# Attention and quantised projection on one core: the max pass leads the exponentials by ten units instead of six, and the query/key projection takes another slot

## The chip, the core and the metric

The kernel runs on one core of one Trainium2 chip. The metric is the time of one execution on the device in microseconds (us), as the median of several runs. The core's engines are TensorE (PE, with its weight loads PEld), VectorE (DVE), ScalarE (ACT), GpSimd (POOL) and SyncE (SP), whose queue here issues every DMA.

## The reference

For each of 16 sequences of 256 tokens with 128 features (float32):

```python
qkv = x @ attn_w.T + attn_b                      # 16 heads of 8, split into q, k, v
scores = einsum("bhki,bhqi->bhkq", k, q) / sqrt(8)
probs = softmax(where(key <= query, scores, -10000), axis=keys)
x = layernorm(x + combine(probs, v) @ out_w.T + out_b)
q_lhs, q_rhs = int8 roundings of x and rhs by absmax / 127
x = layernorm(x + (q_lhs @ q_rhs) * lhs_scale * rhs_scale)
```

## The kernel before

A **batch** b is one sequence. The scores of a batch are made twice on TensorE, in twelve **units** u = 0 to 11 of two or four head pairs and one block of 64 keys each. The **max pass** (`scores_for_max`, bf16, written as M here) puts a unit into one of two PSUM banks `max_bank`; VectorE reduces it (`maxima`, L608), and after the twelfth unit it joins the partial maxima (`join_maxima`, L616). TensorE transposes them (`turn_maxima`, L833), VectorE makes the negated shift of each query from them in three steps (`make_shift`, L632, L638, L641), and SP copies the shift into four extra rows of `q_move` (`load_shift`, L310). The **exp pass** (`scores_for_exp`, written as E) multiplies again with these rows in, into one of three banks `exp_bank`; ScalarE takes the exponential (L453), and TensorE multiplies with the values (`pv`, L819, eight groups 0 to 7).

Queries and keys are split into three bf16 parts so that the score products are accurate. TensorE projects (`project_qk`, L846, into `bank_b`), ScalarE copies the result out twice for each of q and k (`qk_from_psum`, L469: `qk_parts` and `qk_f`, w = 0 and 1), GpSimd subtracts the first part (`split(b, False)`, L393, gives `qk_rest`), VectorE rounds the second part and copies the first one again (`second_part`, L622 and L623), and GpSimd subtracts once more (`split(b, True)`, L397). SP writes the parts to an image in DRAM in two halves (`write_image`, L287) and reads it back in the order that the score products want (`read_image`, L300 and L301). The semaphore `qk_split` counts four steps of a batch.

Behind the attention come `pv_from_psum` (L487), `turn_pv` (L882, into `bank_b`), `normalise` (L651, L655), `turn_heads` (L894), `heads_from_psum` (L494), `project_out` (L902), the first norm, the rounding (`round_z`, L510), `turn_zq` (L915), `zq_from_psum` (L518), `feed_forward` (L923), `scale_ffn` (L703), and the second norm.

The order on each engine is written out by hand. All five engines run the same loop over **phases** b. In phase b, slot u, TensorE issues the max unit `max_unit(b, u)` and the exp unit u of batch b, and behind them what the slot lists; the other engines list their work by the same slots. Each engine takes its own list strictly in order, so an instruction that waits holds back all that stands behind it. With a lead of six, phase b holds units 6 to 11 of the max pass of batch b + 1 in slots 0 to 5 and units 0 to 5 of batch b + 2 in slots 6 to 11. Before the first exp pass come phases -3 to -1 with set-up, ten warm-up matmuls and one more behind each max unit (L941).

Of the kernel before, what the change touches and what calls it, by code (L numbers as in the profile page):

```python
# [46 lines left out]
PARTS = 3  # L47
# [22 lines left out]
HALF = NU // 2  # L70
# [11 lines left out]
def phases(phase, before={}):  # L82

    for b in range(-3, NBATCH + 3):
        if b in before:
            before[b]()
        phase(b)


def max_unit(b, u):  # L90

    return (b + 1, u + HALF) if u < HALF else (b + 2, u - HALF)


def build_program(nc, x, xt, wqkv_t, bqkv, wo_t, bo, rhs_t, out):
    ctx = ExitStack()
    with ctx:
# [30 lines left out]
        ones_b = sb("ones_b", [2, TOK], BF16)  # L128
# [6 lines left out]
        qk_parts = sb("qk_parts", [128, len(PART_SLOTS), TOK], BF16)  # L135

        part = [qk_parts[:, 2 - n:6 + n:3 + 2 * n, :] for n in range(PARTS)]
        first_again = qk_parts[:, 3:5, :]
# [109 lines left out]
        POOL_FIRST = 8 + 2 + (QK_RING - 1) + (QK_RING - 2)  # L248
        POOL_SETUP = POOL_FIRST + 3 * RING
# [5 lines left out]
        def _(sp):  # L255
# [22 lines left out]
            def write_image(b, half):  # L278
# [6 lines left out]
                for w in range(2):  # L285
                    at = RUNS[w][half]
                    sp.dma_start(image[w][b % QK_RING][:, 3 * half:3 * half + 3, :],  # L287
                                 qk_parts[:, at:at + 3, :]).then_inc(image_written[b % QK_RING], 16)
# [62 lines left out]
        def _(pool):  # L351
# [21 lines left out]
            for i in range(1, QK_RING):  # L373
                step(pool.memset(q_move[i][:, :, :].bitcast(F32), 0.0))
            for i in range(2, QK_RING):
                step(pool.memset(k_stat[i][:, :, :, :].bitcast(F32), 0.0))
            assert done[0] == POOL_FIRST, done[0]

# [8 lines left out]
            def split(b, last):  # L387

                if not real(b) or b == 0:
                    return  # L390
                if not last:
                    wait(pool, qk_out, b)
                    pool.tensor_tensor(qk_rest[:, :, :], qk_f[:, :, :], part[0],  # L393
                                       ALU.subtract).then_inc(qk_split[1], 1)
                else:
                    wait(pool, qk_split, b, 3)
                    pool.tensor_tensor(part[2], qk_rest[:, :, :], part[1],  # L397
# [47 lines left out]
        def _(act):  # L445
# [10 lines left out]
            def qk_from_psum(b, w):  # L456
# [8 lines left out]
                for dst in (part[0][:, w, :], qk_f[:, w, :]):  # L465
# [68 lines left out]
            def v_columns_stand():  # L534
# [475 lines left out]
```

## Time and profile before

| what | value |
|---|---|
| median of 3 runs | 300.79 us (300.47 to 301.21) |
| the profiled execution, own time | 302.37 us |
| its span in the trace | 300.7 us |
| granted TensorE clock, mean over the span | 0.962 |
| busy: PE, DVE, ACT, POOL | 248.0, 198.7, 188.5, 112.1 us |

The span is what the trace covers; the execution's own time has 1.67 us more around it. A busy share is an average over a fill, a steady part and a drain. The exp pass of batch 0 starts 40.37 us into the span, that of batch 15 at 266.54 us.

### The profile page before, as it was taken

What the parts mean: (1) busy time and instruction counts of PE and PEld (TensorE: products, weight loads), DVE (VectorE), ACT (ScalarE), POOL (GpSimd) and SP (SyncE); (2) the same over time, 40 slices, a digit from 0 to 9 for tenths busy, and PEclk for the clock granted to TensorE, in tenths of its full rate; (3) what the DMA queues carried; (4) which work ended last, traced back from release to release, by engine and by line L of the source; (5) the groups of instructions that cost most, each with busy time, mean ns of one, the idle gap of its engine ahead of it and who ended that gap; (6) DMA issues with size and microseconds to landing.
All of it is one profiled execution on the core that took longest, in us unless ns stands there. A gap on an engine that the chain in (4) does not pass through costs nothing.

```text
span 300.7 us, 8257 instructions
## 1 busy us (share of the span) xinstructions
PE 248.0 (82%) x3073; PEld 170.2 (57%) x3073; DVE 198.7 (66%) x561; ACT 188.5 (63%) x434; POOL 112.1 (37%) x218
## 2 busy tenths in 40 slices
PE   2389588898989898999899999999998999989410
PEld 1236365666666566666566666666666667655300
DVE  7827558394959685867676767768595978733421
ACT  4023046657677685858594958676777767787441
POOL 7931103123243342525243444443434342433342
PEclk9999899999999999999999999999999999999655
DMA  2356583736373538163815664374636361010000
GB/s 88 109 109 181 118 193 111 142 108 143 109 142 124 143 102 168 65 142 87 197 45 159 109 182 84 127 144 141 125 126 123 127 127 39 2 37 20 19 17 19
DMA packets 51000, 32.72 MB, mean 109 GB/s; under 512 B 7312, under 2 KB 50960, under 8 KB 50960
## 3 DMA queue, kind: packets, MB, share of 16 engines
q1 hardware_dynamic: 50960, 32.19, 43.8%
q8 instruction: 24, 0.39, 0.6%
q14 instruction: 16, 0.13, 0.2%
HBM read 17.17 MB, written 14.68 MB: 106 GB/s over the span
## 4 chain that ended last, share of the span: by engine, by line
PE 26%; SPq 15%; ACT 14%; DMA 14%; DVE 13%; issue 13%; POOL 4%; ACTq 0%; DVEq 0%; POOLq 0%
DMA q_move<-shift 9%; SPq L287 8%; PE exp_bank L776 5%; PE bank_b L846 5%; PE pv_bank L819 4%; ACT probs L453 4%; DVE part_max L608 4%; ACT qk_f L469 3%; PE max_bank L776 3%; PE bank_b L882 3%; ACT heads_t L487 2%; SPq L310 2%; DVE key_max L616 2%; ACT qk_parts L469 2%; DMA k_stat<-imagek 2%
## 5 line engine op out<-in xcount | busy, mean ns | idle before, releaser
L608 DVE TRANSPOSE_TENSOR_REDUCE part_max<-max_bank 128x16 f32<-128x512 f32 (+1 forms) x192 | 119.3, 625 | 69.9 <-PE max_bank L779 65.6
L453 ACT ACTIVATE probs<-exp_bank 128x512 f32<-128x512 f32 (+1 forms) x192 | 102.5, 535 | 74.5 <-PE exp_bank L779 73.1
L776 PE MATMUL exp_bank<-q_move,k_stat 128*128 128x128 bf16 (+3 forms) x512 | 67.5, 234 | 9.1 <-DMA q_move<-shift 9.1
L776 PE MATMUL max_bank<-q_move,k_stat 124*128 124x128 bf16 (+3 forms) x512 | 71.1, 241 | 4.1 <-DMA k_stat<-imagek 3.6
L819 PE MATMUL pv_bank<-probs,v_stat 128*32 128x256 f32 (+3 forms) x1024 | 61.1, 311 | 0.0
L776 PEld LDWEIGHTS max_bank<-q_move,k_stat 124*128 124x128 bf16 x512 | 40.0, 118 | 32.3 <-issue 11.5
L776 PEld LDWEIGHTS exp_bank<-q_move,k_stat 128*128 128x128 bf16 x512 | 41.5, 114 | 15.3 <-DMA q_move<-shift 11.0
L779 PE MATMUL max_bank<-causal,identb 128*128 128x128 bf16 (+1 forms) x192 | 46.3, 241 | 0.0
L779 PE MATMUL exp_bank<-causal,identb 128*128 128x128 bf16 (+1 forms) x192 | 45.5, 237 | 0.0
L393 POOL TENSOR_TENSOR qk_rest<-qk_f,qk_parts 128x512 f32<-128x512 f32 x15 | 17.4, 1159 | 45.2 <-ACT qk_f L469 45.2
L469 ACT ACTIVATE qk_parts<-bank_b,bias 128x256 bf16<-128x256 f32 x32 | 21.3, 665 | 20.6 <-DMA imagek<-qk_parts 16.9
L397 POOL TENSOR_TENSOR qk_parts<-qk_rest,qk_parts 128x512 bf16<-128x512 f32 x15 | 17.4, 1160 | 37.5 <-DVE qk_parts L623 37.5
L819 PEld LDWEIGHTS pv_bank<-probs,v_stat 128*32 128x32 f32 x1024 | 20.2, 108 | 17.3 <-issue 8.8
L415 POOL TENSOR_SCALAR rstd<-moments 128x2 f32<-128x2 f32 x32 | 6.2, 193 | 56.0 <-DVE moments L677 47.6
L428 POOL TENSOR_TENSOR r<-ffn,z 128x256 f32<-128x256 f32 x16 | 11.7, 728 | 36.5 <-DVE ffn L703 36.5
L846 PE MATMUL bank_b<-xt_in,wqkv 128*128 128x256 f32 x64 | 19.3, 428 | 6.0 <-DMA wqkv<-wqkv_dram 3.7
L417 POOL TENSOR_TENSOR rstd<-rstd,minus_half 128x2 f32<-128x2 f32 x32 | 22.6, 705 | 2.7
L469 ACT ACTIVATE qk_f<-bank_b,bias 128x256 f32<-128x256 f32 x32 | 19.9, 623 | 0.0
L527 ACT ACTIVATE o<-r,rstd 128x128 f32<-128x128 f32 x32 | 13.9, 485 | 8.6 <-POOL rstd L421 8.6
L779 PEld LDWEIGHTS max_bank<-causal,identb 128*128 128x128 bf16 x192 | 19.0, 99 | 0.1
L779 PEld LDWEIGHTS exp_bank<-causal,identb 128*128 128x128 bf16 x192 | 18.8, 98 | 0.0
L882 PE MATMUL bank_b<-ident,heads_t 128*128 128x128 f32 x64 | 10.4, 285 | 10.2 <-ACT heads_t L487 10.2
(84 smaller groups left out, 313.4 us busy)
## 6 DMA issues: line engine op xcount, KB each, us to landing
imageq<-qk_parts SPq DMA_DIRECT2D x32, 192.0 KB, 2.1
imagek<-qk_parts SPq DMA_DIRECT2D x32, 192.0 KB, 2.1
q_move<-imageq SPq DMA_DIRECT2D x32, 192.0 KB, 3.7
k_stat<-imagek SPq DMA_DIRECT2D x32, 192.0 KB, 4.2
xt_in<-xt_dram SPq DMA_DIRECT2D x16, 128.0 KB, 4.5
x_in<-x_dram SPq DMA_DIRECT2D x16, 128.0 KB, 4.2
out_dram<-o SPq DMA_DIRECT2D x16, 128.0 KB, 2.0
q_move<-shift SPq DMA_DIRECT2D x32, 8.0 KB
```

What stands on the lines that cost most here:

```text
L287: sp.dma_start(image[w][b % QK_RING][:, 3 * half:3 * half + 3, :], qk_parts[:, at:at + 3, :]).then_inc(image_written[b % QK_RING], 16)
L393: pool.tensor_tensor(qk_rest[:, :, :], qk_f[:, :, :], part[0], ALU.subtract).then_inc(qk_split[1], 1)
L397: pool.tensor_tensor(part[2], qk_rest[:, :, :], part[1], ALU.subtract).then_inc(qk_split[1], 1)
L417: pool.tensor_tensor(t[:, 0, :], t[:, 0, :], minus_half[:, :], ALU.pow).then_inc(made[1], 1)
L453: act.activation(probs[u][:, 0:cols], exp_bank[u % EXP_BANKS][:, 0:cols], ACT.Exp, scale=SCALE).then_inc(exp_done[1], 1)
L469: act.activation(dst, src, ACT.Identity, bias=bias[:, w:w + 1]).then_inc(qk_out[1], 1)
L608: dve.tensor_reduce(o32, max_bank[u % MAX_BANKS][:, 0:n * (TOK - key)].rearrange("k (c q) -> k c q", q=32), op=ALU.max, axis=AX.X, apply_t ...
L776: pe.matmul(tiles[:, j, :], keys, q_move[b % QK_RING][0:rows, p0 + j, key:TOK], start=(j == 0), stop=False, skip_group_check=True)
L779: return pe.matmul(tiles[:, :, 0:KB], identb[:, :], causal[:, :].unsqueeze(1).to_broadcast([128, n, KB]), start=False, stop=True, skip_gro ...
L819: last = pe.matmul(pv_bank[col:col + 32, g, key:TOK], v_stat[b % RING][:, key // KB, p0 + j, :], tiles_of(probs[u], u)[:, j, :], start=(n ...
L846: last = pe.matmul(bank_b[:, w * TOK:(w + 1) * TOK], wqkv[:, w, :], xt_in[b % XT_RING][:, :], start=(w == 0), stop=True, skip_group_check= ...
L882: last = pe.transpose(bank_b[:, c:c + 128], heads_t[:, g, t * 128:(t + 1) * 128], ident[:, :])
```

## The change

The maximum pass leads by ten units: phase b holds units 10 and 11 of batch b + 1 in slots 0 and 1 and units 0 to 9 of batch b + 2 behind them. `turn_maxima` moves from slot 7 to 2, `make_shift` to slots 3 and 4. `project_qk` moves from slot 0 (for batch b + 3) to slot 9 (for b + 4), its copies on ScalarE to slots 10 and 11, `second_part` on VectorE from slot 6 to slot 0 of the next phase. `qk_parts` exists twice. The second copy of the first part (L623) moves from VectorE to GpSimd, and `second_part` waits for it (`qk_split` 2 of 4). SP's list is re-ordered. The rows of ones in `k_stat` come by one DMA for each of the four buffers, from a tile that GpSimd prepares, instead of four each. Other slots move as shown. The cut diff:

```diff
-HALF = NU // 2
+LEAD = 10
...
-    for b in range(-3, NBATCH + 3):
+    for b in range(-4, NBATCH + 3):
...
-    return (b + 1, u + HALF) if u < HALF else (b + 2, u - HALF)
+    ahead, unit = divmod(u + LEAD, NU)
+    return b + 1 + ahead, unit
...
-        ones_b = sb("ones_b", [2, TOK], BF16)
+        shift_on = sb("shift_on", [128, 2, TOK], BF16)
...
-        qk_parts = sb("qk_parts", [128, len(PART_SLOTS), TOK], BF16)
-
-        part = [qk_parts[:, 2 - n:6 + n:3 + 2 * n, :] for n in range(PARTS)]
-        first_again = qk_parts[:, 3:5, :]
+        qk_parts = [sb(f"qk_parts{i}", [128, len(PART_SLOTS), TOK], BF16) for i in range(2)]
+
+        part = [[qk_parts[i][:, 2 - n:6 + n:3 + 2 * n, :] for n in range(PARTS)] for i in range(2)]
+        first_again = [qk_parts[i][:, 3:5, :] for i in range(2)]
...
-        POOL_FIRST = 8 + 2 + (QK_RING - 1) + (QK_RING - 2)
-        POOL_SETUP = POOL_FIRST + 3 * RING
+        POOL_FIRST = 14
+        POOL_ROWS = POOL_FIRST + 2 * (QK_RING - 2)
+        POOL_SETUP = POOL_ROWS + 3 * RING
...
+            def set_shift_rows(slots):
+
+                for i in slots:
+                    sp.dma_start(k_stat[i][SHIFT_ROW:DEPTH, :, :, :],
+                                 shift_on[SHIFT_ROW:DEPTH, :, :].unsqueeze(1).to_broadcast([4, PAIRS, 2, TOK])).then_inc(ones_loaded, 16)
+
             def rows_stand():
 
-                sp.wait_ge(rows_set, 3)
-                load_ones((0, 1))
-                sp.wait_ge(pool_setup, 1)
+                sp.wait_ge(rows_set, 2)
+                sp.wait_ge(pool_setup, POOL_FIRST)
+                set_shift_rows((0, 1))
 
             def last_rows_stand():
-                sp.wait_ge(pool_setup, POOL_FIRST)
-                load_ones(range(2, QK_RING))
-
-            def load_ones(slots):
-
-                for i in slots:
-                    for s in range(2):
-                        for row in (SHIFT_ROW + s, SHIFT_ROW + 2 + s):
-                            sp.dma_start(k_stat[i][row:row + 1, :, s, :],
-                                         ones_b[0:1, :].unsqueeze(1).to_broadcast([1, PAIRS, TOK])).then_inc(ones_loaded, 16)
+                sp.wait_ge(pool_setup, POOL_ROWS)
+                set_shift_rows(range(2, QK_RING))
 
             def phase(b):
-                load_xt(b + 4)
                 load_x(b)
                 write_image(b + 3, 0)
-                store(b - 3)
                 write_image(b + 3, 1)
                 load_shift(b + 1)
+                load_xt(b + 5)
                 read_image(b + 3)
-
-            phases(phase, {-3: rows_stand, -2: last_rows_stand})
+                store(b - 3)
+
+            phases(phase, {-3: rows_stand, -1: last_rows_stand})
...
+            step(pool.memset(shift_on[:, :, :], 0.0))
+            for row in (SHIFT_ROW, SHIFT_ROW + 2):
+                step(pool.affine_select(out=shift_on[:, :, :], in_=shift_on[:, :, :], compare_op=ALU.not_equal, fill=1.0,
+                                        base=-row, pattern=[[-1, 2], [0, TOK]], channel_multiplier=1))
+            step(pool.memset(q_move[1][:, :, :].bitcast(F32), 0.0))
             assert done[0] == POOL_FIRST, done[0]
+
+            def last_rows():
+                for i in range(2, QK_RING):
+                    step(pool.memset(q_move[i][:, :, :].bitcast(F32), 0.0))
+                    step(pool.memset(k_stat[i][:, :, :, :].bitcast(F32), 0.0))
+                assert done[0] == POOL_ROWS, done[0]
...
+                first, second, third = part[b % 2]
                 if not last:
                     wait(pool, qk_out, b)
-                    pool.tensor_tensor(qk_rest[:, :, :], qk_f[:, :, :], part[0],
+                    wait(pool, qk_split, b - 1)
+                    pool.tensor_tensor(qk_rest[:, :, :], qk_f[:, :, :], first,
                                        ALU.subtract).then_inc(qk_split[1], 1)
+                    pool.tensor_copy(first_again[b % 2], first).then_inc(qk_split[1], 1)
...
+                norm_factors(b - 2, 0, y_made, rstd_made)
+                split(b + 3, True)
                 add_residual(b - 3)
-                split(b + 3, False)
+                add_bias(b - 1)
                 norm_factors(b - 3, 1, r_stats, rstd2_made)
-                split(b + 3, True)
-                add_bias(b - 1)
-                norm_factors(b - 1, 0, y_made, rstd_made)
-
-            phases(phase, {-2: rest_of_setup, 1: sum_stands})
+                split(b + 4, False)
+
+            phases(phase, {-3: last_rows, -1: rest_of_setup, 1: sum_stands})
...
-                    wait(act, qk_split, b - 1)
-                    wait_ring(act, image_written, b - 1, 4, 4)
+                    wait(act, qk_split, b - 1, 1)
+                    wait_ring(act, image_written, b - 2, 4, 4)
...
+                if b == 0:
+                    act.wait_ge(pool_setup, POOL_SETUP)
...
-                    if u == 1:
-                        qk_from_psum(b + 3, 0)
+                    if u == 0:
+                        zq_from_psum(b - 3)
                     if u == 2:
-                        qk_from_psum(b + 3, 1)
+                        norm1(b - 2)
                     if u == 3:
                         pv_from_psum(b - 1)
                     if u == 4:
-                        norm1(b - 2)
-                    if u == 5:
                         v_from_psum(b + 1)
-                    if u == 6:
-                        norm2(b - 3)
                     if u == 7:
+                        round_z(b - 2)
+                    if u == 8:
                         heads_from_psum(b - 1)
                     if u == 9:
-                        round_z(b - 2)
+                        norm2(b - 3)
+                    if u == 10:
+                        qk_from_psum(b + 4, 0)
                     if u == 11:
-                        zq_from_psum(b - 2)
-
-            phases(phase, {-1: v_columns_stand})
+                        qk_from_psum(b + 4, 1)
+
+            phases(phase)
...
-                    wait(dve, qk_split, b, 1)
-                    dve.tensor_copy(part[1], qk_rest[:, :, :]).then_inc(qk_split[1], 1)
-                    dve.tensor_copy(first_again, part[0]).then_inc(qk_split[1], 1)
-
+                    wait(dve, qk_split, b, 2)
+                    dve.tensor_copy(part[b % 2][1], qk_rest[:, :, :]).then_inc(qk_split[1], 1)
...
-                    if u == HALF:
+                    maxima(*max_unit(b, u))
+                    if u == 0:
+                        first_sum(b - 2, 2)
+                        if b > -3:
+                            second_part(b + 3)
+                    if u == 1:
                         join_maxima(b + 1)
-                    maxima(*max_unit(b, u))
-                    if u == 0 and b == -2:
-                        second_part(b + 3)
-                    if u == 1:
+                    if u == 2:
                         scale_ffn(b - 3)
                     if u == 3:
+                        make_shift(b + 1, 0)
+                        make_shift(b + 1, 1)
+                    if u == 4:
+                        make_shift(b + 1, 2)
+                        scales(b - 2, 0)
+                    if u == 5:
                         second_stats(b - 3, 0)
-                    if u == 4:
+                        scales(b - 2, 1)
+                    if u == 6:
+                        normalise(b - 1, 0)
                         second_stats(b - 3, 1)
-                    if u == 5:
-                        normalise(b - 1, 0)
-                        scales(b - 2, 0)
+                        scales(b - 2, 2)
                         normalise(b - 1, 1)
-                    if u == 6:
-                        scales(b - 2, 1)
-                        if b >= -1:
-                            second_part(b + 3)
-                    if u == 7:
-                        make_shift(b + 1, 0)
-                        scales(b - 2, 2)
-                        make_shift(b + 1, 1)
-                    if u == 8:
-                        make_shift(b + 1, 2)
-                    if u == 9:
+                    if u == 10:
                         first_sum(b - 1, 0)
-                    if u == 10:
+                    if u == 11:
                         first_sum(b - 1, 1)
-                    if u == 11:
-                        first_sum(b - 1, 2)
...
-                if real(b - 2):
-                    wait(pe, normed, b - 2)
-                else:
+                if real(b + 2):
                     wait(pe, qk_out, b + 2)
+                else:
+                    wait(pe, normed, b - 3)
...
+                if real(b - 5):
+                    wait(pe, normed, b - 5)
+                elif real(b - 3):
...
-                if real(b + 4):
-                    wait(pe, qk_out, b + 4)
-                elif real(b + 1):
-                    wait(pe, shift_made, b + 1)
+                if real(b + 2):
+                    wait(pe, shift_made, b + 2)
...
-                    if b == -2 and u == HALF:
-                        setup()
-                        warm_up(WARM)
                     scores_for_max(*max_unit(b, u))
                     scores_for_exp(b, u)
-                    if b == -1 or (b == -2 and u >= HALF):
+                    if b == -1 or (b == -2 and u >= NU - LEAD):
                         warm_up(1)
                     if u == 0:
                         pv(b - 1, 5)
-                        feed_forward(b - 3)
-                        project_qk(b + 3)
                     if u == 1:
                         pv(b - 1, 6)
+                        feed_forward(b - 3)
                     if u == 2:
+                        turn_maxima(b + 1)
                         pv(b - 1, 7)
                     if u == 3:
                         project_v(b + 1)
-                    if u == 4:
+                    if u == 5:
                         turn_pv(b - 1)
-                    if u == 5:
                         pv(b, 0)
                     if u == 6:
                         pv(b, 1)
+                    if u == 7:
                         turn_heads(b - 1)
-                    if u == 7:
-                        turn_maxima(b + 1)
                         pv(b, 2)
-                    if u == 8:
+                    if u == 9:
                         project_out(b - 1)
-                    if u == 9:
+                        project_qk(b + 4)
                         pv(b, 3)
                     if u == 10:
                         pv(b, 4)
                     if u == 11:
                         turn_zq(b - 2)
 
+            def setup_and_warm_up():
+                setup()
+                warm_up(WARM)
+
             pe.wait_ge(w_in, 16)
-            phases(phase)
+            phases(phase, {-2: setup_and_warm_up})
```

## Rows read from the trace of the kernel before

**Rows 1.** The page, first part: busy us (share) xinstructions of each engine.
```profile
PE 248.0 (82%) x3073; PEld 170.2 (57%) x3073; DVE 198.7 (66%) x561; ACT 188.5 (63%) x434; POOL 112.1 (37%) x218
```
**Rows 2.** Waits, 100 to 235 us: who <- for whom: us, times, longest.
```profile
PE bank_b L882 <- ACT heads_t L487: 6.5, 9, 0.7
PE exp_bank L776 <- DMA q_move<-shift: 5.4, 8, 1.0
```
**Rows 3.** Timeline of PE: start us, us; first exp units of batches 1, 12, 13, 14.
```profile
52.71 0.41 PE L776 MATMUL exp_bank<-q_move,k_stat 128*128 128x256 bf16 x2 [0.87 <-DMA q_move<-shift]
...
225.51 0.41 PE L776 MATMUL exp_bank<-q_move,k_stat 128*128 128x256 bf16 x2 [0.56 <-DMA q_move<-shift]
...
241.36 0.41 PE L776 MATMUL exp_bank<-q_move,k_stat 128*128 128x256 bf16 x2 [0.69 <-DMA q_move<-shift]
...
254.51 0.38 PE L776 MATMUL exp_bank<-q_move,k_stat 128*128 128x256 bf16 x2
```
**Rows 4.** The chain of waits, 144 to 179 us: start us, us, what.
```profile
147.84 0.92 PE bank_b L846 x4
```
**Rows 5.** Timeline of PE: from `turn_zq` to group 7 of `pv`.
```profile
254.01 0.38 PE L915 MATMUL bank_a<-ident,zq 128*128 128x128 f32 x2
...
257.03 0.32 PE L819 MATMUL pv_bank<-probs,v_stat 128*32 128x64 f32 x8
```
**Rows 6.** Timeline: exp of a last unit; copies of keys; GpSimd's first subtraction.
```profile
60.20 0.64 PE L819 MATMUL pv_bank<-probs,v_stat 128*32 128x256 f32 x8
...
60.37 0.38 ACT L453 ACTIVATE probs<-exp_bank 128x256 f32<-128x256 f32 x1 [0.80 <-PE exp_bank L779]
60.65 0.77 ACT L480 ACTIVATE v_stat<-bank_a 64x256 f32<-64x256 f32 x2
...
150.99 0.86 ACT L469 ACTIVATE qk_parts<-bank_b,bias 128x256 bf16<-128x256 f32 x1
...
151.55 0.77 ACT L469 ACTIVATE qk_f<-bank_b,bias 128x256 f32<-128x256 f32 x1
...
152.40 1.16 POOL L393 TENSOR_TENSOR qk_rest<-qk_f,qk_parts 128x512 f32<-128x512 f32 x1 [1.31 <-ACT qk_f L469]
```
**Rows 7.** Timeline of DVE, 154 to 158 us.
```profile
154.12 0.45 DVE L608 TRANSPOSE_TENSOR_REDUCE part_max<-max_bank 128x8 f32<-128x256 f32 x1 [1.11 <-PE max_bank L779]
...
155.01 0.41 DVE L655 TENSOR_TENSOR heads<-bank_b,rden 128x256 f32<-128x256 f32 x1
...
155.34 0.60 DVE L616 TENSOR_REDUCE key_max<-part_max 128x64 f32<-128x256 f32 x1
...
156.72 0.41 DVE L622 CAST qk_parts<-qk_rest 128x512 bf16<-128x512 f32 x1
...
157.05 0.29 DVE L623 COPY qk_parts<-qk_parts 128x512 bf16<-128x512 bf16 x1
```
**Rows 8.** Timeline of POOL: two operations with one input.
```profile
3.13 0.29 POOL L367 TENSOR_SCALAR_AFFINE_SELECT ident<-ident 128x128 f32<-128x128 f32 x1 [0.23 <-POOL minus_half L365]
...
153.64 0.19 POOL L415 TENSOR_SCALAR rstd<-moments 128x2 f32<-128x2 f32 x1
```
**Rows 9.** Timeline: the copy of the heads; one max unit to `turn_heads`.
```profile
157.54 0.38 ACT L494 ACTIVATE heads_d<-bank_a 128x256 f32<-128x256 f32 x1
...
247.63 0.41 PE L776 MATMUL max_bank<-q_move,k_stat 124*128 124x256 bf16 x2
...
248.76 0.44 PE L894 MATMUL bank_a<-ident,heads 128*128 128x128 f32 x2
```
**Rows 10.** Timeline of the fill: warm-up matmuls around TensorE's longest wait; GpSimd's filling of `v_stat`.
```profile
11.45 2.99 POOL L381 MEMSET v_stat<- 128x1024 f32 x3
...
29.83 0.38 PE L941 MATMUL exp_bank<-warm 128*128 128x512 bf16 x1
33.78 0.41 PE L776 MATMUL max_bank<-q_move,k_stat 124*128 124x256 bf16 x2 [3.58 <-DMA k_stat<-imagek]
...
35.47 0.63 PE L941 MATMUL exp_bank<-warm 128*128 128x512 bf16 x1
```

More of the change, by code:

```diff
@@ L287, in write_image @@
                     sp.dma_start(image[w][b % QK_RING][:, 3 * half:3 * half + 3, :],
-                                 qk_parts[:, at:at + 3, :]).then_inc(image_written[b % QK_RING], 16)
+                                 qk_parts[b % 2][:, at:at + 3, :]).then_inc(image_written[b % QK_RING], 16)
             def read_image(b):
@@ L372, in _ @@
                                         base=0, pattern=[[-1, KB]], channel_multiplier=1))
[L373 to L376, printed above, removed]
-            assert done[0] == POOL_FIRST, done[0]
+            step(pool.memset(shift_on[:, :, :], 0.0))
[3 more added lines that the diff above has]
+            step(pool.memset(q_move[1][:, :, :].bitcast(F32), 0.0))
+            assert done[0] == POOL_FIRST, done[0]
+            def last_rows():
[3 more added lines that the diff above has]
+                assert done[0] == POOL_ROWS, done[0]
             def rest_of_setup():
@@ L390, in split @@
                     return
+                first, second, third = part[b % 2]
                 if not last:
                     wait(pool, qk_out, b)
-                    pool.tensor_tensor(qk_rest[:, :, :], qk_f[:, :, :], part[0],
+                    wait(pool, qk_split, b - 1)
+                    pool.tensor_tensor(qk_rest[:, :, :], qk_f[:, :, :], first,
                                        ALU.subtract).then_inc(qk_split[1], 1)
+                    pool.tensor_copy(first_again[b % 2], first).then_inc(qk_split[1], 1)
                 else:
                     wait(pool, qk_split, b, 3)
-                    pool.tensor_tensor(part[2], qk_rest[:, :, :], part[1],
+                    pool.tensor_tensor(third, qk_rest[:, :, :], second,
                                        ALU.subtract).then_inc(qk_split[1], 1)
@@ L461, in qk_from_psum @@
                     wait(act, qk_proj, b)
-                    wait(act, qk_split, b - 1)
-                    wait_ring(act, image_written, b - 1, 4, 4)
+                    wait(act, qk_split, b - 1, 1)
+                    wait_ring(act, image_written, b - 2, 4, 4)
                 src = bank_b[:, w * TOK:(w + 1) * TOK]
-                for dst in (part[0][:, w, :], qk_f[:, w, :]):
+                for dst in (part[b % 2][0][:, w, :], qk_f[:, w, :]):
                     if w == 1:
@@ L532, in _ @@
             act.wait_ge(bias_in, 16)
-            def v_columns_stand():
-                act.wait_ge(pool_setup, POOL_SETUP)
             def phase(b):
@@ L568, in _ @@
             dve.memset(warm[:, :].bitcast(F32), 0.0).then_inc(warm_zeroed, 1)
-            dve.memset(ones_b[:, :], 1.0).then_inc(rows_set, 1)
             for i in range(2):
@@ L572, in _ @@
             dve.memset(part_max[:, :, :], MASKED).then_inc(rows_set, 1)
-            dve.wait_ge(rows_set, 4)
+            dve.wait_ge(rows_set, 3)
             def rhs_scales():
@@ L745, in phase @@
-                    if u == 8:
-                        make_shift(b + 1, 2)
-                    if u == 9:
+                    if u == 10:
                         first_sum(b - 1, 0)
-                    if u == 10:
+                    if u == 11:
                         first_sum(b - 1, 1)
-                    if u == 11:
-                        first_sum(b - 1, 2)
-            first = 0
             rhs_scales()
-            wait(dve, qk_out, first)
-            dve.tensor_tensor(qk_rest[:, :, :], qk_f[:, :, :], part[0],
+            wait(dve, qk_out, 0)
@@ L759, in _ @@
+            dve.tensor_tensor(qk_rest[:, :, :], qk_f[:, :, :], part[0][0],
                               ALU.subtract).then_inc(qk_split[1], 1)
-            second_part(first)
-            wait(dve, qk_split, first, 3)
-            dve.tensor_tensor(part[2], qk_rest[:, :, :], part[1],
+            dve.tensor_copy(first_again[0], part[0][0]).then_inc(qk_split[1], 1)
+            second_part(0)
+            wait(dve, qk_split, 0, 3)
+            dve.tensor_tensor(part[0][2], qk_rest[:, :, :], part[0][1],
@@ L798, in scores_for_exp @@
                     if b == 0:
-                        pe.wait_ge(ones_loaded, 16 * 4 * QK_RING)
+                        pe.wait_ge(ones_loaded, 16 * QK_RING)
                     pe.wait_ge(shift_loaded, 32 * (b + 1))
@@ L827, in turn_maxima @@
                 wait(pe, max_joined, b)
-                if real(b - 2):
-                    wait(pe, normed, b - 2)
+                if real(b + 2):
+                    wait(pe, qk_out, b + 2)
                 else:
-                    wait(pe, qk_out, b + 2)
+                    wait(pe, normed, b - 3)
                 for s in range(2):
@@ L840, in project_qk @@
                 wait_ring(pe, xt_loaded, b, 1)
-                if real(b - 3):
+                if real(b - 5):
+                    wait(pe, normed, b - 5)
+                elif real(b - 3):
                     wait(pe, shift_made, b - 3)
```

## The prediction

> **What bounds the kernel now.** I read the page first: TensorE is the busiest engine with 82% of the span, VectorE has 66% [rows 1]. A share over fill and drain says little, so I took the waits of the steady part next. TensorE has two kinds of wait there: for the shift rows that SP copies, just ahead of each exp pass (5.4 us in 8 times), and for ScalarE's copy ahead of `turn_pv` (6.5 us in 9 times) [rows 2]. Then I measured a phase by the start of its first exp unit: phase 12 takes 225.51 to 241.36 = 15.85 us; phases 1 to 11 take (225.51 - 52.71) / 11 = 15.71 each; phase 13, the first with nothing to project for queries and keys, takes 254.51 - 241.36 = 13.15 [rows 3]. In phase 13 TensorE hardly waits. The projection costs TensorE 0.92 [rows 4]. So TensorE's own work is 13.15 + 0.92 = 14.07 us a phase, and 1.6 us of each full phase are waits. That is what any re-ordering can win: some 12 x 1.6 = 20 us. The reader is to see that the kernel sits close to the bound of one engine whose list is taken in order: whatever it waits for is paid in full.
>
> **What the change takes away.** The maxima of batch b + 1 are joined in slot 1 of phase b, the shift is made by slot 4 and needed a phase later, so the wait for the shift rows goes. `turn_pv` waited because `qk_from_psum` stood in front of `pv_from_psum` on ScalarE (its wait on `qk_out`); these copies are now in slots 10 and 11, so that wait goes as well. If nothing took their place the phase would be 14.07.
>
> **What the change puts in their place.** Follow the parts of batch b + 3. ScalarE ends their copies in slot 11 of phase b - 1; GpSimd then subtracts and copies; VectorE's `second_part` stands in slot 0 of phase b, behind one max unit, and waits for both (`qk_split` 2). Queued behind it on VectorE are the reduction of max unit 11 and `join_maxima`, and TensorE's `turn_maxima` in slot 2 waits for the join. The chain, from the moment TensorE has issued exp unit 11:
> - ScalarE takes its exponential 0.17 later and is free for the next instruction after 0.28 (60.20, 60.37, 60.65); the first copy of the keys holds it 0.56 (150.99 to 151.55), the second lasts 0.77 [rows 6]: 1.78.
> - GpSimd starts 0.08 later and subtracts for 1.16 [rows 6]: 3.02.
> - GpSimd's copy of 512 bf16 elements is not in the trace. One-input operations take 0.19 for 2 elements and 0.29 for 128 [rows 8], 0.8 ns an element, so 0.60 for 512. Bounds: 0.29 (the one with a quarter of the elements) and 1.16 (the two-input one of the same size). I take 0.60, since it has one input: 3.62.
> - VectorE starts some 0.07 later, the cast holds it 0.33 (156.72 to 157.05), the reduction of unit 11 takes 0.45, the join 0.60 with 0.03 ahead of it [rows 7]: 5.10. TensorE starts 0.08 later: 5.18.
>
> In that time TensorE has `turn_zq`, three max and three exp units, two groups of `pv` and the feed-forward product: before, the same list takes 257.03 - 254.01 = 3.02 [rows 5]; with the somewhat larger max units that now fall there 3.1. So TensorE stands 5.18 - 3.1 = 2.1 us at `turn_maxima` in every phase from 0 to 12. A copy of 0.29 makes it 1.8, one of 1.16 makes it 2.6. The loop closes on itself: a later `turn_maxima` makes the next exp unit 11 later too, so nothing catches up.
>
> The GPSIMD Engine Reference of the Trainium skill, section on engine selection, says elementwise work belongs on VectorE and that GpSimd is slower, near line rate only with one input; that speaks against the moved copy. VectorE's copy takes 0.29 [rows 7], against my 0.60. By the same page's best case for a one-input loop, 512 elements in about 0.77 us, which no row here shows, the stall would be 2.2 to 2.3 and the whole 2 us more.
>
> **Smaller waits that come up.** `turn_heads` (slot 7) waits for VectorE's `heads`, made in slot 6. Before, from the start of the reduction to the end of `heads` it is 155.42 - 154.12 = 1.30 [rows 7], with one other operation between; after, the reduction is the 512-column one, 0.27 longer, and two small ones replace the other: 1.6, and with 0.31 ahead and 0.08 behind 2.0 us. TensorE covers it with an exp unit, a `pv` group, a smaller max unit and an exp unit: the first three take about 1.1 [rows 9], with the fourth 1.55. Stall 0.45. `project_out` (slot 9) waits for `heads_d`, which ScalarE now makes behind exponential 8 with nothing else on TensorE in slot 8: 0.3 + 0.38 for the exponential + 0.38 for the copy [rows 9] + 0.06 = 1.12 against 0.75 of TensorE's work: 0.4. `project_v` (slot 3) waits for `scale_ffn`, behind the delayed join: 0.1. Together 0.95 a phase, bounds 0 (all three covered) and 1.3.
>
> **Costed at nothing.** SP's new order: the image of a batch is written 3 to 6 us after the stall, read some 2 us later, and needed a phase later, about 6 us of cover; `store` at the end of the phase only holds back loads due later. The single DMAs for the ones, the tile behind them and the double `qk_parts` act in the fill. The four max units taken out of phases 14 and 15 give back 1.1 us.
>
> **Fill.** TensorE's wait of 3.58 for the second image [rows 10] shrinks, since the second batch's parts no longer wait for the first image. But `second_part` of batch 2 stands in front of max unit 11 of batch 0, so that TensorE waits from about 29.5 to 32.7; and GpSimd fills `v_stat` (2.99 [rows 10] and six small ones, 4.2) before the third part of batch 2, whose image lands only near 45.5. These times are estimates, the list of the fill gone through with the same durations. With the chain above once more in phase 0 the first exp unit of batch 1 moves from 52.71 to 56.3: +3.6, bounds 0 and +6.
>
> **The sum**, against the span of 300.7. A full phase: 14.07 + 2.1 + 0.95 = 17.1. Fill +3.6. Phases 1 to 11: 11 x 17.1 - 0.5 (no feed-forward in phase 1) = 187.6 against 172.8: +14.8. Phase 12: 17.1 - 0.92 = 16.2 against 15.85: +0.3. Phase 13: +0.9. Phases 14, 15 and the drain: -1.1. Together +18.5: span 319.2, its own time 1.67 more, 320.9. The profiled execution's 302.37 stands 1.6 over the median of the runs, 300.79, so the median becomes 319.3.
>
> **Rivals.**
> - *TensorE-bound, faster.* If the chain were hidden, the phase would be 14.07 + 0.95 = 15.0: fill +1.5, phases 1 to 11 -8, phase 12 -1.8, rest -0.2: 292; without the small waits 281. For it: both old waits do go. Against: the phase gets shorter only if the stall is under 15.71 - 15.0 = 0.7, the chain under 3.8 us; ScalarE's part, GpSimd's subtraction, the reduction and the join alone are 1.78 + 1.16 + 0.45 + 0.60 = 3.99, without the copy, the cast and every hand-over. Chance 0.10.
> - *Break-even.* The chain near 3.8 to 4.2 us, with some of the smaller waits gone: within 1 us of 300.8, or a few us over. 0.04 for the same.
> - *The clock falls.* A stall of about 1 us before each exp pass left the clock at 2.4 GHz; behind the wait of 3.58 a warm-up matmul takes 0.63 where it took 0.38 [rows 10], and it stays so for some 3 us, which costs about 1.6. My stalls of 2.1 lie between. If each did this: 12 x 1.6 = +19, 338. The skill's page TensorE: Matmul & The Clock Gate, section on oscillation, describes such a kernel that starts cold in each of its tiles; by it the time would be this 338 if the stall were long enough. 0.08.
> - *The small waits are covered*, the main stall stays: 319.3 - 12 = 307. This is the low side of the forecast.
>
> **Chances and range.** The stall at `turn_maxima`, clock kept: 0.78, from 304 (no small waits, a fill that loses nothing) to 329 (copy at 1.16, fill +6). The 0.10, 0.04 and 0.08 are the rest. Within 0.3% is what a measurement of this kernel can tell from no change. Slower 0.86, same 0.04, faster 0.10.
>
> **What the trace after would show.** Right: a wait of TensorE's `turn_maxima` for `join_maxima`, 2 us, once a phase; VectorE idle ahead of its cast for GpSimd's copy, 1.5 to 2 us; no wait for the shift rows; phases of 17.1. Wrong: phases near 14 to 15, with GpSimd's pair ending before VectorE gets to the cast; or matmuls at half speed behind each stall; or waits for the images.

## Result, and the profile after

The changed kernel takes 336.32 us (median of 4 runs, 335.71 to 337.17) against 300.89 for the kernel before on the same chip: ratio 1.118, 95% interval 1.115 to 1.121. The profiled execution spans 334.7 us. The forecast was slower, 319.3 us, in a range of 304 to 329: the direction and the place of the stall are right, the size is not.

The page of the changed kernel, first its busy shares and then the granted clock in 40 slices. Line numbers below are those of the changed kernel and of each experiment; they stand a few lines from those of before. TensorE's share falls from 82% [rows 1] to 79% though its busy time rises from 248.0 to 264.2 us on the same work. Some 10 us of that rise lie in the stretches at a lower clock, the sixes to eights in the clock's row: a phase with one keeps TensorE busy for 15.9 to 16.1 us, the others for 14.7.

```profile
PE 264.2 (79%) x3075; PEld 179.0 (53%) x3077; DVE 195.7 (58%) x545; ACT 189.3 (57%) x434; POOL 123.8 (37%) x236
...
PEclk9999769999998989997979999897979799999955
```

The waits of the changed kernel from 100 to 260 us (who <- for whom: us, times, longest). The two waits of [rows 2] are gone. In their place stands `turn_maxima` (L835) waiting for the join, and under it VectorE's cast (L630) waiting for GpSimd's copy.

```profile
DVE qk_parts L630 <- POOL qk_parts L404: 16.7, 8, 2.1
PE bank_b L835 <- DVE key_max L624: 14.0, 8, 1.8
PE bank_a L904 <- ACT heads_d L506: 3.7, 9, 0.4
PE bank_a L925 <- ACT zq_t L530: 1.7, 8, 0.2
PE bank_a L896 <- DVE heads L661: 1.4, 9, 0.2
PE bank_a L867 <- DVE ffn L709: 1.0, 5, 0.2
```

The timeline of the changed kernel from the end of exp unit 11 to `turn_maxima` (start us, us). The first row's start is the moment at which unit 11 has been issued; the rows behind it are the links of the predicted chain in order.

```profile
147.15 0.38 PE L917 MATMUL bank_a<-ident,zq 128*128 128x128 f32 x2
147.47 0.40 ACT L463 ACTIVATE probs<-exp_bank 128x256 f32<-128x256 f32 x1
147.73 0.86 ACT L479 ACTIVATE qk_parts<-bank_b,bias 128x256 bf16<-128x256 f32 x1
148.29 0.78 ACT L479 ACTIVATE qk_f<-bank_b,bias 128x256 f32<-128x256 f32 x1
149.15 1.16 POOL L402 TENSOR_TENSOR qk_rest<-qk_f,qk_parts 128x512 f32<-128x512 f32 x1 [6.62 <-ACT qk_f L479]
150.26 0.61 POOL L404 COPY qk_parts<-qk_parts 128x512 bf16<-128x512 bf16 x1
150.90 0.43 DVE L630 CAST qk_parts<-qk_rest 128x512 bf16<-128x512 f32 x1 [2.09 <-POOL qk_parts L404]
151.24 0.44 DVE L616 TRANSPOSE_TENSOR_REDUCE part_max<-max_bank 128x8 f32<-128x256 f32 x1
151.72 0.58 DVE L624 TENSOR_REDUCE key_max<-part_max 128x64 f32<-128x256 f32 x1
152.36 0.34 PE L835 MATMUL bank_b<-ident,key_max 128*64 128x64 f32 x4 [1.75 <-DVE key_max L624]
```

The chain is 152.36 - 147.15 = 5.21 us; 5.18 was worked out. GpSimd's copy is 0.61 against 0.60.

What was not in the sum comes right behind it. The windows of the changed kernel (stretch, busy us of each engine, PEclk, DMA share, GB/s), in the same phase:

```profile
147.10:152.30 5.20, 3.29 (x47) 2.18 (x43) 3.06 (x9) 3.65 (x9) 2.90 (x5) 1.00 0.10 31
152.30:154.50 2.20, 1.95 (x35) 1.49 (x36) 2.06 (x7) 1.72 (x4) 2.11 (x5) 0.94 0.45 164
154.50:157.90 3.40, 3.40 (x29) 2.60 (x28) 2.08 (x8) 1.76 (x5) 0.71 (x2) 0.54 0.38 125
157.90:165.00 7.10, 6.53 (x78) 4.48 (x78) 3.47 (x10) 3.68 (x9) 1.28 (x4) 1.00 0.74 148
```

For 3.4 us TensorE is at 1.2 GHz (PEclk 0.54, as the row's edges are a little off that stretch) and busy all the time. Two rows of its timeline show a pair of matmuls of one shape, ahead of the stall and in that stretch:

```profile
145.42 0.35 PE L778 MATMUL max_bank<-q_move,k_stat 124*128 124x192 bf16 x2
...
154.45 0.51 PE L778 MATMUL max_bank<-q_move,k_stat 124*128 124x192 bf16 x2
```

The stall is 1.75 us in each of phases 3 to 12. In phases 1 and 2 it is longer:

```profile
63.31 0.34 PE L835 MATMUL bank_b<-ident,key_max 128*64 128x64 f32 x4 [2.30 <-DVE key_max L624]
...
80.50 0.34 PE L835 MATMUL bank_b<-ident,key_max 128*64 128x64 f32 x4 [2.33 <-DVE key_max L624]
```

The exp pass, by the first exp unit of each batch: the start of batch 1 (us from the span's start), then lengths in us.

| | before | after | sum of the prediction |
|---|---|---|---|
| batch 1 | 52.71 | 58.51 | 56.3 |
| phases 1 to 11, each | 15.71 | 18.18 | 17.1 |
| phase 12 | 15.85 | 17.57 | 16.2 |
| phase 13 | 13.15 | 14.43 | 14.05 |
| batch 14 to the end | 46.2 | 44.2 | 45.1 |

The phases after are of two kinds: 17.1 to 17.5 us where the clock stays, 18.4 to 18.8 where one stretch of 3.4 us runs at 1.2 GHz. The second kind is 7 of phases 1 to 11 (3, 4, 6, 7, 9, 10 and 11); phase 12 has such a stretch too. Phases 1 and 2, with the longest stalls, have none.

### The profile page after: what moved, and what is told of

The parts are those of the page before. It is cut to its first block, busy times and chain, and to the rows that moved or that the text cites. A ratio compares the mean times of both kernels' runs of the same rounds, so it can differ in the third digit from the quotient of the medians.

```text
span 334.7 us, 8270 instructions
## 1 busy us (share of the span) xinstructions
PE 264.2 (79%) x3075; PEld 179.0 (53%) x3077; DVE 195.7 (58%) x545; ACT 189.3 (57%) x434; POOL 123.8 (37%) x236
## 3 DMA queue, kind: packets, MB, share of 16 engines
HBM read 17.17 MB, written 14.68 MB: 95 GB/s over the span
## 4 chain that ended last, share of the span: by engine, by line
PE 48%; DVE 14%; ACT 12%; issue 11%; POOL 10%; DMA 2%; SPq 1%; ACTq 0%; DVEq 0%; POOLq 0%
PE max_bank L778 9%; PE pv_bank L821 8%; PE exp_bank L778 6%; POOL qk_rest L402 4%; PE bank_b L850 4%; ACT qk_f L479 4%; PE bank_a L867 4%; PE bank_a L904 4%; ACT qk_parts L479 3%; DVE part_max L616 3%; PE bank_b L884 3%; PE exp_bank L781 3%; DVE key_max L624 2%; PE max_bank L781 2%; POOL qk_parts L404 2%
## 5 line engine op out<-in xcount | busy, mean ns | idle before, releaser
L616 DVE TRANSPOSE_TENSOR_REDUCE part_max<-max_bank 128x16 f32<-128x512 f32 (+1 forms) x192 | 117.3, 620 | 76.8 <-PE max_bank L781 74.3
L778 PE MATMUL max_bank<-q_move,k_stat 124*128 124x128 bf16 (+3 forms) x512 | 74.9, 250 | 4.1 <-DMA k_stat<-imagek 3.4
L778 PE MATMUL exp_bank<-q_move,k_stat 128*128 128x128 bf16 (+3 forms) x512 | 70.7, 244 | 0.0
L402 POOL TENSOR_TENSOR qk_rest<-qk_f,qk_parts 128x512 f32<-128x512 f32 x15 | 17.4, 1158 | 115.0 <-ACT qk_f L479 114.9
L778 PEld LDWEIGHTS max_bank<-q_move,k_stat 124*128 124x128 bf16 x512 | 38.3, 119 | 37.5 <-issue 15.5
L781 PE MATMUL max_bank<-causal,identb 128*128 128x128 bf16 (+1 forms) x192 | 48.1, 251 | 0.0
L781 PE MATMUL exp_bank<-causal,identb 128*128 128x128 bf16 (+1 forms) x192 | 47.4, 247 | 0.0
L778 PEld LDWEIGHTS exp_bank<-q_move,k_stat 128*128 128x128 bf16 x512 | 44.3, 118 | 4.7 <-issue 2.5
L425 POOL TENSOR_SCALAR rstd<-moments 128x2 f32<-128x2 f32 x32 | 8.7, 271 | 72.9 <-DVE moments L724 51.1
L630 DVE CAST qk_parts<-qk_rest 128x512 bf16<-128x512 f32 x16 | 9.1, 568 | 28.8 <-POOL qk_parts L404 28.8
L835 PE MATMUL bank_b<-ident,key_max 128*64 128x64 f32 x64 | 5.6, 257 | 25.0 <-DVE key_max L624 24.9
L513 ACT ACTIVATE z<-y,rstd 128x128 f32<-128x128 f32 x32 | 14.0, 487 | 19.4 <-POOL rstd L431 19.4
L407 POOL TENSOR_TENSOR qk_parts<-qk_rest,qk_parts 128x512 bf16<-128x512 f32 x15 | 17.4, 1160 | 3.6 <-DVE qk_parts L630 3.5
```

The source lines that it names most:

```text
L402: pool.tensor_tensor(qk_rest[:, :, :], qk_f[:, :, :], first, ALU.subtract).then_inc(qk_split[1], 1)
L407: pool.tensor_tensor(third, qk_rest[:, :, :], second, ALU.subtract).then_inc(qk_split[1], 1)
L513: act.activation(z[b % RING][:, t, :], y[:, t, :], ACT.Identity, bias=rstd[0][:, 1, t:t + 1], scale=rstd[0][:, 0, t:t + 1]).then_inc(z_mad ...
L616: dve.tensor_reduce(o32, max_bank[u % MAX_BANKS][:, 0:n * (TOK - key)].rearrange("k (c q) -> k c q", q=32), op=ALU.max, axis=AX.X, apply_t ...
L778: pe.matmul(tiles[:, j, :], keys, q_move[b % QK_RING][0:rows, p0 + j, key:TOK], start=(j == 0), stop=False, skip_group_check=True)
L781: return pe.matmul(tiles[:, :, 0:KB], identb[:, :], causal[:, :].unsqueeze(1).to_broadcast([128, n, KB]), start=False, stop=True, skip_gro ...
```

## Experiments

All are edits of the changed kernel that leave out none of its work. Each is timed beside the kernel before, which has 301.13 us beside the late `second_part`, the eight matmuls, the copy back and the small waits, and 301.03 beside the other four. "Undisturbed" is a phase without a stretch at 1.2 GHz.

**`second_part` two slots later** (`e1_second_late`).

```diff
 # VectorE
                     if u == 0:
                         first_sum(b - 2, 2)
-                        if b > -3:
+                        if b == -2:
                             second_part(b + 3)
...
                     if u == 2:
                         scale_ffn(b - 3)
+                        if b > -2:
+                            second_part(b + 3)
```

> The changed kernel with one edit: second_part moves from slot 0 to the end of slot 2 on VectorE (in the fill phase -2 it stays). Theory A (the stall of TensorE at turn_maxima, 1.8 us a phase, comes from second_part standing in front of the reduction of unit 11 and of the join; the clock falls only because of that stall): no wait of turn_maxima over 0.2 us, granted clock near 0.96, full phases of 15.0 to 15.2 us where the changed kernel has 17.4 to 18.8, time 290 to 298 us. Theory B (the ten-unit lead itself costs the time, through banks or shared engines): phases stay over 16.5 us and the time over 312 us.

311.5 us, ratio 1.034 (1.032 to 1.036). `turn_maxima` no longer waits at all, and from batch 1 to the drain no stretch is at 1.2 GHz; phases are 16.25 us. So both the stall and the clock hang on the place of this one call: 25 us of the 35 that the change costs. But 16.25 is 1.05 over theory A's 15.2, and the time misses its 298 by 13.5. The waits of this kernel, 100 to 240 us:

```profile
PE bank_b L886 <- ACT heads_t L499: 6.2, 8, 0.8
PE bank_a L906 <- ACT heads_d L506: 3.7, 9, 0.4
PE bank_a L927 <- ACT zq_t L530: 1.9, 9, 0.2
PE bank_a L898 <- DVE heads L661: 1.3, 8, 0.2
```

The wait for `heads_t` that the prediction struck off is back with 0.8 us a phase, once the larger stall no longer covers it.

**The stall filled with matmuls** (`e2_busy_stall`). Eight matmuls on a zero tile run while `turn_maxima` waits for the join, which comes no earlier.

```diff
 # turn_maxima(b)
+                if real(b + 2):
+                    wait(pe, qk_out, b + 2)
+                    for _ in range(8):
+                        pe.matmul(bank_b[:, :], warm[:, 0:128], warm[:, :], start=True, stop=True)
                 wait(pe, max_joined, b)
```

> The changed kernel with eight matmuls on a zero tile (some 1.7 us) in front of turn_maxima's wait for the join, into a bank that is free there; the stall itself stays. Theory A (behind the stall the granted clock falls to 1.2 GHz for 3.4 us in most phases, and that costs some 1.3 us each time): no stretch at half clock in the steady part, all full phases near 17.4 us, time 323 to 328 us, 8 to 13 us under the changed kernel, although work is added. Theory B (the slow matmuls are not due to the idle time): the stretches stay and the time is 336 us or more.

329.17 us, ratio 1.091 (1.087 to 1.095) against 1.118 for the changed kernel: 7 us less for 112 matmuls more; theory A's band of 323 to 328 is missed by one. From phase 3 on all full phases take 17.5 us. Timeline and windows of this kernel; the window's PEclk column is 1.00 in each phase:

```profile
149.71 1.89 PE L832 MATMUL bank_b<-warm 128*128 128x512 bf16 x8
151.64 0.34 PE L839 MATMUL bank_b<-ident,key_max 128*64 128x64 f32 x4
```
```profile
112.00:129.50 17.50, 16.44 (x201) 10.85 (x199) 11.14 (x35) 11.64 (x28) 7.00 (x13) 1.00 0.48 116
129.50:147.00 17.50, 16.45 (x202) 10.86 (x200) 11.14 (x34) 11.65 (x28) 7.00 (x13) 1.00 0.46 115
147.00:164.50 17.50, 16.44 (x201) 10.85 (x199) 11.13 (x34) 11.64 (x29) 7.01 (x13) 1.00 0.46 115
```

So the idle time in front of `turn_maxima` is what lowers the clock. The lower clock costs 200.0 - 191.9 = 8.1 us over phases 1 to 11 and 17.57 - 16.62 = 0.95 in phase 12.

**Four matmuls in its place** (`e7_half_busy`, the same edit with `range(4)`).

> As e2_busy_stall, with four zero matmuls instead of eight, so that about 0.9 us of idle time is left in front of turn_maxima's matmuls. Theory A (the clock falls for the length of the idle stretch, and one of about 1 us, as the kernel before had in each phase, is harmless): no half-clock stretch in the steady part, within 2 us of e2_busy_stall's 329 us. Theory B (any idle stretch there is enough now and then): some stretches stay, 331 to 336 us.

327.43 us, ratio 1.088 (1.086 to 1.090), phases of 17.49 us, no stretch at 1.2 GHz in the steady part: theory A. Of the 1.7 us under the kernel with eight, 1.6 are in the fill, where batch 1 starts at 58.37 and not at 60.01. TensorE's idle time ahead of `turn_maxima` is 7.1 us in 8 times, 0.9 each, and the clock stays up, as it did with the 0.7 to 1.0 of the kernel before [rows 2]. In phases 1 and 2 it is 1.44 and 1.47, and the clock stays up there too.

**The copy back on VectorE** (`e3_copy_back`).

```diff
 # GpSimd, split(b, False)
-                    pool.tensor_copy(first_again[b % 2], first).then_inc(qk_split[1], 1)
...
 # VectorE, second_part(b)
-                    wait(dve, qk_split, b, 2)
+                    wait(dve, qk_split, b, 1)
                     dve.tensor_copy(part[b % 2][1], qk_rest[:, :, :]).then_inc(qk_split[1], 1)
+                    dve.tensor_copy(first_again[b % 2], part[b % 2][0]).then_inc(qk_split[1], 1)
```

> The changed kernel with the second copy of the first part made on VectorE again, behind the cast, and second_part waiting only for GpSimd's subtraction. Theory A (everything in the chain counts in full): the chain is 0.61 us shorter on GpSimd and 0.25 longer on VectorE, so the stall goes from 1.8 to about 1.4 us and phases at full clock from 17.4 to 17.0; with half-clock stretches as frequent as in the changed kernel 331 us, with none 319 us. Theory B (the copy on GpSimd is the cause of the loss): the stall is under 0.5 us and the time under 310 us.

324.24 us, ratio 1.076 (1.072 to 1.081), between theory A's two ends. The stall is 1.40 us as expected, undisturbed phases are 17.13 for 17.0. In the profiled execution 3 of phases 1 to 12 have a stretch at 1.2 GHz, where it was 8: phases 1 and 2, whose stalls are longer, and of the ten with 1.40 us one, phase 12. The 0.35 us that the chain lost (0.6 less on GpSimd, the copy more on VectorE) come off the stall in full, and with the fewer slow stretches the copy back is worth 12 us of the 35. It is a part of the cause and not the main one: theory B's 0.5 us and 310 us are far off.

```profile
61.53 0.34 PE L834 MATMUL bank_b<-ident,key_max 128*64 128x64 f32 x4 [1.93 <-DVE key_max L623]
...
79.69 0.34 PE L834 MATMUL bank_b<-ident,key_max 128*64 128x64 f32 x4 [1.99 <-DVE key_max L623]
...
166.30 0.34 PE L834 MATMUL bank_b<-ident,key_max 128*64 128x64 f32 x4 [1.40 <-DVE key_max L623]
```

**The small waits covered as well** (`e4_late_and_small`), on top of the first experiment.

```diff
 # TensorE, slot 7 and slot 9
-                        turn_heads(b - 1)
                         pv(b, 2)
+                        turn_heads(b - 1)
...
-                        project_out(b - 1)
                         project_qk(b + 4)
+                        project_out(b - 1)
```

> As e1_second_late, and in TensorE's list turn_heads moves behind group 2 of pv in slot 7, project_out behind project_qk in slot 9. Theory A (turn_heads waits 0.45 and project_out 0.4 us a phase, for work that other matmuls can cover): full phases of 14.2 to 14.4 us, 8 to 11 us under e1_second_late, so 281 to 288 us. Theory B (those waits are hidden elsewhere, the phase is held by another loop): within 2 us of e1_second_late.

299.94 us, ratio 0.996 (0.994 to 0.997), the same as the kernel before. Phases are 15.27 us against 16.25: covering the two waits is worth 1.0 us a phase and 11.6 in all, as theory A said, but its 14.2 to 14.4 a phase and 281 to 288 us are missed, since it took no account of the wait for `heads_t`. Of a phase of 15.27 that wait is 0.78 and the one for `zq_t` 0.21. The chain of `heads_t`, in this kernel's timeline:

```profile
137.98 0.19 POOL L431 TENSOR_SCALAR rstd<-rstd 128x2 f32<-128x2 f32 x1
...
138.21 0.88 ACT L513 ACTIVATE z<-y,rstd 128x128 f32<-128x128 f32 x2 [1.39 <-POOL rstd L431]
...
139.36 0.58 ACT L499 ACTIVATE heads_t<-pv_bank 128x512 f32<-128x512 f32 x1
...
140.00 0.66 PE L886 MATMUL bank_b<-ident,heads_t 128*128 128x128 f32 x4 [0.78 <-ACT heads_t L499]
```

`norm1` in ScalarE's slot 2 waits 1.39 us for GpSimd's norm factors, and `pv_from_psum` stands behind it. On GpSimd these factors stand behind the subtraction and the copy.

**The norm factors first on GpSimd** (`e5_norm_first`), on top of that; `second_part` moves a slot further.

```diff
 # GpSimd, phase(b)
                 norm_factors(b - 2, 0, y_made, rstd_made)
+                split(b + 3, False)
+                add_residual(b - 3)
                 split(b + 3, True)
-                add_residual(b - 3)
                 add_bias(b - 1)
                 norm_factors(b - 3, 1, r_stats, rstd2_made)
-                split(b + 4, False)
 # VectorE: second_part(b + 3) behind make_shift in slot 3
```

> As e4_late_and_small (phases of 15.3 us, 0.8 of them TensorE's wait for heads_t), with GpSimd's list changed: norm_factors of batch b - 2 stands ahead of split(b + 3, False) instead of behind it, add_residual ahead of split(b + 3, True); second_part moves on to the end of slot 3. Theory A (ScalarE stands at norm1 for the factors that wait on GpSimd behind the two operations on the query and key parts, and the copy heads_t behind norm1 is late by that): no wait for heads_t, full phases of 14.3 to 14.6 us, time 283 to 290 us. Theory B (the copy heads_t is late for another reason): the wait for heads_t stays at 0.7 us or more, time 297 to 302 us.

291.78 us, ratio 0.969 (0.967 to 0.971). The wait for `heads_t` is gone, phases are 14.68 us; this bears out theory A's reason, though time and phases miss its bands by 2 and 0.1 us. The waits of 100 to 240 us left on TensorE are small:

```profile
PE bank_a L927 <- ACT zq_t L530: 1.9, 9, 0.2
PE bank_b L886 <- DVE shift L647: 1.8, 9, 0.2
```

**`feed_forward` a slot later** (`e8_feed_forward`), on top of that (in slot 2, ahead of `turn_maxima`).

> As e5_norm_first, and feed_forward moves from the end of slot 1 to slot 2, behind the score units and ahead of turn_maxima. Theory A (its wait of 0.2 us a phase for zq_t is covered there and the result is still in time for project_v): 2 to 3 us under e5_norm_first. Theory B (scale_ffn on VectorE then comes late for project_v and takes the gain back): within 1 us of e5_norm_first.

290.54 us, ratio 0.966 (0.963 to 0.968). The wait for `zq_t` goes, but `turn_pv` now waits 0.4 for `shift` where it waited 0.2, and the phase stays at 14.68. So the gain is taken back, as theory B has it, though by way of the shift and not of `project_v`. The times are 1.2 us apart, outside both theories' bands, and the two sets of runs overlap (290.85 to 292.29, 289.89 to 291.49); of the 0.65 us between the two spans 0.62 are in the fill (batch 2 starts at 69.78 and not at 70.40). Both kernels beat the kernel before by 3%.

**GpSimd's filling of `v_stat` a phase earlier** (`e6_early_v_fill`), on top of the first experiment (`-2: rest_of_setup` in place of `-1`).

> As e1_second_late (311.5 us), with GpSimd's filling of v_stat ahead of its phase -2 instead of phase -1, so that it no longer stands between the two subtractions of batch 2. Theory A (the late image of batch 2 holds TensorE in phase 0 of the exp pass): the first exp unit of batch 1 starts at 53 to 55 us instead of 58.1, everything behind it moves by the same, 307 to 309 us. Theory B (the fill is held by something else): within 1 us of e1_second_late.

307.69 us, ratio 1.023 (1.021 to 1.024), 3.8 us under the first experiment; batch 1 starts at 54.71 and not at 58.09, and all behind it moves along: theory A.

## Why the prediction failed

**The step that failed is the rival of the clock.** The prediction put the stall of 2.1 us between 1 us, which left the clock alone, and 3.58, which did not, gave the fall 0.08 and left it out of sum and range. A stall of 1.75 us did lower it, in 8 of the ten phases 3 to 12, for 3.4 us each time, while the stalls of 2.30 and 2.33 us in phases 1 and 2 did not. The price is 9.1 / 8 = 1.1 us a time (1.0 to 1.3) where 1.6 was said, since the matmuls shown take 0.51 for 0.35 us, not twice as long. Over phases 1 to 12 that is 9.1 us rather than 0 or 19. It is shown by filling the stall with matmuls: the stretches go, and 7 us with them, or 9 with half as many matmuls. Without them the time is 329.17 or 327.43 us, at the high side of the forecast.

**The chain at `turn_maxima`: right.** 5.21 us against 5.18, each link within 0.1 but the first, 0.32 from the issue of unit 11 to its exponential against 0.17. The stall is 1.75, not 2.1: the feed-forward product ahead of it now waits 0.21 us for `zq_t` out of the same time, and TensorE's work in it is 5.21 - 1.75 - 0.21 = 3.25 and not 3.1. That the place of `second_part` makes it is shown by moving the call. The loop that feeds on itself is seen in the phases: the copy taken off GpSimd shortened each undisturbed phase by 0.35 us; nothing caught up.

**The small waits: right in place and sum; TensorE's own work was too small.** `heads_d` 0.41 a phase (forecast 0.4), `heads` 0.16 (0.45), `ffn` 0.2 (0.1), `zq_t` 0.21 (none): 0.98 against 0.95. Yet undisturbed phases are 17.4 to 17.5 against 17.1, some 4 us over phases 1 to 11. The term that was short is the 14.07, phase 13 plus one row of the projection. One full phase each of the kernel before, the changed kernel, and the experiments with the late `second_part` and with the small waits covered (same columns as above, PE's busy time first):

```profile
209.81:225.51 15.70, 14.43 (x190) 10.26 (x191) 11.45 (x35) 11.61 (x27) 6.33 (x13) 1.00 0.54 128
130.23:147.71 17.48, 14.70 (x193) 10.11 (x191) 11.12 (x34) 11.64 (x28) 7.01 (x13) 1.00 0.47 115
154.51:170.76 16.25, 14.66 (x193) 10.12 (x190) 11.39 (x34) 11.39 (x28) 6.86 (x13) 1.00 0.51 125
163.90:179.17 15.27, 14.25 (x192) 10.30 (x191) 11.38 (x34) 11.39 (x28) 6.86 (x13) 1.00 0.55 132
```

TensorE is busy for 14.43 us in a phase before, so that its waits there were 1.3 us and not 1.6, and for 14.70 after; with 2.74 of waits that gives 17.44. Covering the waits for `heads` and `heads_d` took away 0.57 us of idle time and 0.41 of busy time (14.66 to 14.25): a wait costs more than the idle time shown for it. Where the busy time goes with it was not looked into.

**The wait for `heads_t`: the reason was incomplete.** The prediction struck it off since ScalarE's query and key copies had moved away. With the stall gone it is back, through GpSimd's factors and `norm1`. In the changed kernel the stall hid it, so it is no part of the 336 us. The rival of 292 us left it out: with the stall gone, the first experiment takes 311.5.

**Fill: +5.8 and not +3.6.** The image of batch 2 landed when it was said to (timeline of the changed kernel):

```profile
33.18 0.34 PE L835 MATMUL bank_b<-ident,key_max 128*64 128x64 f32 x4 [2.75 <-DVE key_max L624]
...
45.35 0.61 PE L778 MATMUL max_bank<-q_move,k_stat 124*128 124x256 bf16 x2 [2.89 <-DMA k_stat<-imagek]
```

32.7 and 45.5 had been estimated. From just before the end of the second wait the clock is at 1.2 GHz for 6.8 us, and the matmuls there take 0.61 where they take 0.41 [rows 10]; how much of the missing 2.2 us that makes was not tried, and the kernel with four filling matmuls, with one such stretch of 3.4 us in phase 0, starts batch 1 only 0.1 earlier. `rest_of_setup` between the two subtractions of batch 2 is 3.4 us of the fill, as shown by moving it in the kernel with the late `second_part`.

**The sum from end to end**: 319.2 forecast, 334.7 measured. Fill +2.2; clock in phases 1 to 12 +9.1; the rest of phases 1 to 12 +4.7 (0.63 us a phase more of busy time, 0.31 less of waits); phase 13 +0.4; the end -0.9: together 15.5.

**The gain.** With `second_part` late, the small waits covered and the factors first, the same ten-unit lead gives 14.68 us a phase against 15.71. The lead was not the cost. Whether a lead of six with the same order of work would gain as much was not tried. Of the loss of 35 us, some 25 hang on one call in a slot that comes before its input exists.

## What to carry to other kernels

Where every engine works through a fixed list, write for each moved call when its input exists, in the units of the busiest engine, and place it behind that moment; a call one slot too early blocks all that stands behind it, whatever slack its own result has. Price an idle stretch on TensorE twice: once for itself and once for the chance that the matmuls behind it run at half clock, which in this kernel was there from 1.4 us a phase on. When the largest wait is taken out, look at the trace again before summing the gain: the next one (here `heads_t`) was hidden under it.

## What the runs showed of the hardware that was not expected

The granted clock did not answer to the length of the idle stretch by a yes or no. Ahead of `turn_maxima`, in phases 1 to 12:

| idle | kernel | phases | with a stretch at 1.2 GHz |
|---|---|---|---|
| 2.30, 2.33 us | changed | 2 | 0 |
| 1.93, 1.99 | copy back on VectorE | 2 | 2 |
| 1.75 | changed | 10 | 8 |
| 1.44, 1.47 | four matmuls | 2 | 0 |
| 1.40 | copy back on VectorE | 10 | 1 |
| 0.9 | four matmuls | 10 | 0 |
| 0 to 0.6 | eight matmuls | 12 | 0 |

These are counts of one profiled execution each. The longest stalls left the clock up and shorter ones did not, so the length alone does not decide. The Trainium skill's page TensorE: Matmul & The Clock Gate, section on oscillation, tells of a kernel that starts cold in every one of its tiles; here the trace shows it in some phases and not in others of the same length of stall, so its cost is neither that of all nor that of none. What decides which phase is hit was not tried.

GpSimd's copy of 512 bf16 elements took 0.61 us. The GPSIMD Engine Reference of the Trainium skill, section Elementwise — side-by-side cycle accounting, gives 768 ns for 512 elements as the best case of its loop; the measured copy is shorter.
